# A graph network kernel: one of the dense half-chunks is done in another place of the first layers

## The chip, the cores and the metric

The kernel runs on one core of a Trainium2 chip. It is one program with five instruction streams: VectorE (DVE), ScalarE (ACT), TensorE (PE), GpSimd (POOL) and SyncE (SP). The metric is device time in microseconds, the median over runs; less is better.

## The reference

`x` has 100000 rows of 32 numbers; 25000 edges (`src`, sorted `dst`, a type each) touch some of them. Four layers follow, each `x = x + layer(relu(layernorm(x)))`.

```python
h = relu(layernorm(x)); x = x + norm * (segment_sum((norm * h)[dst], src) + norm * h)      # norm = rsqrt(1 + out degree)
h = relu(layernorm(x)); x = x + sum_k theta[k] * L^k h                                     # L h = h - D^-1/2 A D^-1/2 h, k = 0..4
h = relu(layernorm(x)); x = x + relu(sum over edges of gate * message + self term)         # typed messages, at dst
h = relu(layernorm(x)); x = x + ten steps of 0.9 * norm * segment_sum((h * norm)[src], dst) + 0.1 * h
```

A node that no edge touches has no neighbours, so all four layers act on its row alone: three layer norms (the third with its factor for the last layer) and three additions. This is the *dense* part. The kernel computes it for all 100000 rows, and afterwards overwrites the rows that have edges.

## The kernel before

**Dense part.** The rows are cut into a small tail and 20 chunks of 128 partitions by 39 rows (1248 numbers, 0.64 MB). Two chunks make a *half*, and there are ten halves, numbered 0 to 9. `dense_half` on VectorE (with `dense_pair`, lines 1311 to 1357) does three rounds of the same layer norm: sum, centre, [ScalarE squares, L2135], sum of squares, [ScalarE roots, L2138], reciprocal, scale, add. ScalarE also issues a half's two loads and, as its chunks are done, its two stores (`dense_halves` of ScalarE, L2149 to L2166). ScalarE loads one half ahead within a group of halves: it waits for the stores of half n - 1, issues the loads of half n + 1, and only then does the squares and roots of half n. The first load of a group is issued when VectorE raises `dense_go`.

**Where the halves are.** The halves are put by hand into the order of the irregular work:

- *early* (0 to `MIDDLE_HALF` - 1), after the tail: while GpSimd scatters the sums of nodes with many edges (L1902) and then gathers the source rows `xs` (L1896), with at most four source gathers in flight.
- *middle* (up to `ROUNDS_HALF` - 1), after `dense_go` at L1447: while GpSimd gathers own and first rows of the listed edges.
- *rounds* (up to `LATE_HALF` - 1): one after the second `l1_step` (L1504, L1505), one after the last step (L1511).
- *late* (from `LATE_HALF` on), in another tile, after L1514.

**Between early and middle.** `source_norm(part)` and `first_layer` compute the first layer for three parts of the source rows (columns 0 to 104, 104 to 150, 150 to 196), and each waits for its part's gathers. After each part SyncE stores its own rows (L527). Then come two listings, the clear at L1422 and L1423 that lets GpSimd gather own rows, a layer norm, the first rows (stored by SyncE at L530), and `Z`, the rows that SyncE stores as x_rows (L548). VectorE waits for the store of the first rows and for the store of x_rows (`s2_stored`); the latter because it clears the third rows' tile `m3_f`, a part of `z_t`, which that store reads. It computes the coefficients `cf` (L618 and L1443 here) and goes on to the middle halves.

**After the middle.** VectorE takes own and first rows, makes the carried sums (scan L1214), lists again (`compact_listed`) and raises `l1_second_ready` (L1473). SyncE stores the second and the own listed rows, GpSimd gathers 14 columns of each, and VectorE goes on at L1480 and L1482. Three `l1_step`s follow; the first two end in a store of third rows and 14 gathers of them, with half of a scatter of 50 columns of finished rows behind each.

All waits are on semaphores and each engine's order is the order of the code; no planner moves anything.

Of the kernel before, what the change touches and what calls it, by code (L numbers as in the profile page):

```python
# [69 lines left out]

UNROLL = 4
TURNS = DCHUNKS // UNROLL
MIDDLE_HALF, ROUNDS_HALF, LATE_HALF, HALVES = 3, 5, 7, 2 * TURNS


def build(nc, x, src, dst, etype, theta, w_basis, w_comp, w_self, a1t, a1b, a2t, a2b, rel, out):
# [12 lines left out]
    V, S, T, G = nc.vector, nc.scalar, nc.tensor, nc.gpsimd  # L89
# [20 lines left out]
    with ctx:  # L110
        def sb(name, cols, dt=f32, parts=P):
            return ctx.enter_context(nc.sbuf_tensor(name, [parts, cols], dt))

        def sem(name):
            return ctx.enter_context(nc.semaphore(name))
# [89 lines left out]
        small = sb("small", 4)  # L205
# [44 lines left out]
        EARLY_IN, LATE_IN, MIDDLE_IN, ROUNDS_IN = range(4)  # L250
# [39 lines left out]
        m3_f = z_t[:, 5 * CW2:6 * CW2]  # L290
# [141 lines left out]
        s = {n: sem(n) for n in SEMS}  # L432
# [22 lines left out]
        def bc(ap, n=D):  # L455
            return ap.unsqueeze(2).to_broadcast([ap.shape[0], ap.shape[1], n])

        def bf(ap, n=EC):
            return ap.unsqueeze(1).to_broadcast([ap.shape[0], n, ap.shape[1]])
# [150 lines left out]
        def _(dve):  # L610
            link = Chain(dve, s["dve"])
            marks.clear()

            def tt(o, a, b, op):
                return V.tensor_tensor(o, a, b, op)  # L615

            def ts(o, a, s1, s2, op0, op1=None):
                return V.tensor_scalar(o, a, s1, s2, op0, op1) if op1 is not None else V.tensor_scalar(o, a, s1, None, op0)  # L618
# [594 lines left out]
            def sums_of(chain, w, m, z, cont, carry_in, number):  # L1213
                chain.many([V.tensor_tensor_scan(z[:, :, f], cont, m[:, :, f], 0.0, ALU.mult, ALU.add) for f in range(D)])  # L1214
                V.tensor_copy(last_row, z[:, w - 1, :]).then_inc(s[carry_in], 1)
                dve.wait_ge(s[carry_in], number)
# [132 lines left out]
            def turn_half(i, h, chain, place):  # L1349
                dve.wait_ge(s[f"dense_in{h}"], 32 * i + 32)  # L1350
                dense_pair([2 * h, 2 * h + 1], P, DCH, chain, lambda l, b: 12 * i + (3 + 6 * h + 2 * l + b + 1), place)

            def dense_half(n, place):
                turn_half(n // 2, n % 2, Chain(dve, s["dense_chain"], tail_chain.n + n * PER // 2), place)

            def dense_halves(first, last, place):
                for n in range(first, last):
                    dense_half(n, place)
                dve.wait_ge(s["dense_done"], 2 * last + 1)
# [71 lines left out]
            dve.wait_ge(s["s2_ready"], 1)  # L1431
            dve.wait_ge(s["l1_first_ready"], 1)
            dve.wait_ge(s["l1_first_stored"], 16)
            dve.wait_ge(s["s2_stored"], 16)
            link(V.memset(m3_f, 0.0))

            th = [theta_sb[:, k:k + 1] for k in range(L1_STEPS + 1)]
            cf = [coef[:, k:k + 1] for k in range(2 * L1_STEPS)]
# [7 lines left out]
            dve.wait_ge(s["l1_own_stored"], 16 * len(XS_PARTS))  # L1446
            V.memset(small[:, 2:3], 0.0).then_inc(s["dense_go"], 1)  # L1447
            dense_halves(MIDDLE_HALF, ROUNDS_HALF, MIDDLE_IN)
            dve.wait_ge(s["l1_own_in"], 16 * W1)
            x1c = OWN1[:, :, 0:D]  # L1450
            link(V.tensor_copy(disc, OWN1[:, :, D]))
# [15 lines left out]
            with dve.If(longest <= XW):  # L1467
                ch = Chain(dve, s["l1c_chain"])
                w2 = W2S["l1"]
                m2, own2, m3, z2, t2, u2 = (a[:, 0:w2, :] for a in (M2, OWN2, M3, Z2, T2, U2))  # L1470
                cn2, hd2, ds2 = (a[:, 0:w2] for a in (cont2, head2, dis2))

                V.tensor_copy(small[:, 2:3], small[:, 1:2]).then_inc(s["l1_second_ready"], 1)  # L1473
                V.scalar_tensor_tensor(out=x1c, in0=Zc, scalar=cf[0], in1=x1c, op0=ALU.mult, op1=ALU.add).then_inc(s["l1_listed_ready"], 1)
                dve.wait_ge(s["l1_listed_ready"], 1)
                ch(ts(valid1, SECOND[:, :, D], FAR / 2, FAR, ALU.is_lt, ALU.mult))
                ch(tt(nohome, nohome, valid1, ALU.add))
                ch(tt(homei, OWN1[:, :, D + 2], nohome, ALU.add))
                dve.wait_ge(s["l1_second_in"], 16 * w2)
                ch(V.tensor_copy(pf3[:, 0:w2], m2[:, :, D]))  # L1480
                dve.wait_ge(s["l1_listed_in"], 16 * w2)
                ch(V.tensor_copy(ds2, own2[:, :, D]))  # L1482
                O2 = own2[:, :, 0:D]
                base_n = ch.n
                PER2 = 1 + 4

                def l1_step(i, m):
                    ch = Chain(dve, s["l1c_chain"], base_n + i * PER2)
                    sums_of(ch, w2, m, z2, cn2, "l1c_carry_in", i + 1)
                    dve.wait_ge(s["l1c_carry_out"], i + 1)  # L1490
                    ch(tt(t2, bf(CAR, w2), bc(hd2), ALU.mult))
                    ch(tt(z2, z2, t2, ALU.add))
                    ch(tt(z2, z2, bc(ds2), ALU.mult))
                    if i < L1_STEPS - 2:
                        tt(u2, z2, bc(ds2), ALU.mult).then_inc(s["l1_third_ready"], 1)
                    ch(V.scalar_tensor_tensor(out=O2, in0=z2, scalar=cf[i + 1], in1=O2, op0=ALU.mult, op1=ALU.add))
                    assert ch.n == PER2

                l1_step(0, m2)
                for i in range(1, L1_STEPS - 1):  # L1500
                    dve.wait_ge(s["l1_third_in"], 16 * w2 * i)
                    l1_step(i, m3)
                    if i == 1:
                        V.memset(small[:, 2:3], 0.0).then_inc(s["dense_go"], 1)  # L1504
                        dense_half(ROUNDS_HALF, ROUNDS_IN)  # L1505
                ch = Chain(dve, s["l1c_chain"], base_n + (L1_STEPS - 1) * PER2)
                ch(tt(home2i[:, 0:w2], own2[:, :, D + 2], away2[:, 0:w2], ALU.add))
                V.tensor_copy(small[:, 2:3], small[:, 3:4]).then_inc(s["x2c2_ready"], 1)

                V.memset(small[:, 1:2], 0.0).then_inc(s["s_final"], 1)  # L1510
                dense_half(ROUNDS_HALF + 1, ROUNDS_IN)  # L1511
                dve.wait_ge(s["dense_done"], 2 * LATE_HALF + 1)
                dve.wait_ge(s["s_final"], 1)
                V.memset(small[:, 2:3], 0.0).then_inc(s["dense_go"], 1)  # L1514
                dense_halves(LATE_HALF, HALVES, LATE_IN)
# [741 lines left out]
        def _(pe):  # L2257
# [37 lines left out]
            def place(layout, wo, nv):  # L2295
                for g, (cut, hot, _, given) in enumerate(layout):
                    n = cut.stop - cut.start
                    placed[0] += 1
                    pe.wait_ge(s["place_in"], placed[0])
                    for q in range(n):  # L2300
                        ins = T.matmul(PLACED[:, 0:2 * nv * wo], hot[:, q, :], given[:, q, :, :].rearrange("p d c -> p (d c)"),
                                       start=g == 0 and q == 0, stop=g == len(layout) - 1 and q == n - 1)
                    ins.then_inc(s["place_out"], 1)
# [133 lines left out]
```

## Time and profile before

| | |
|---|---|
| median of 3 runs | 2403.41 us (2403.01 to 2404.06) |
| the profiled execution's own time | 2400.89 us |
| its span, first to last instruction | 2399.1 us |
| VectorE busy | 1839.2 us, 77% of the span |
| GpSimd busy | 1445.9 us, 60% |
| ScalarE, TensorE busy | 386.9 us, 336.3 us |

The page also has the chain of work that ended last. Here it covers the end of the program, from 1967 us on, mostly GpSimd's gathers and scatters. The stages that the diff touches lie between 600 and 1560 us; they are read in the timelines, where each row has a start (us from the span's start), a duration, the engine, the line of the code, the operation with its tiles, and in brackets how long the engine had been idle before it and what released it. A line such as L615 or L1896 is a helper's, so the tile tells which work it is.

### The profile page before, as it was taken

Reading aid. Unit: us, or ns where it says so; the run is one execution under the profiler, and the core shown is the slowest. Engines: PE = TensorE matmul, PEld = TensorE weight load, DVE = VectorE, ACT = ScalarE, POOL = GpSimd, SP = SyncE. Lnnn points to the kernel's source line nnn. Section 1 sums busy time; section 2 is a strip of 40 time slices with the busy share of each in tenths; the row PEclk is TensorE's granted clock in tenths of the full one; section 3 lists DMA queues with packets and bytes.
Section 4 is the critical chain, followed back from the end, with each engine's and each line's share of the span. In section 5 each row is a group of like instructions: output and inputs, shape, how many; then the busy total and the mean of one; then the engine's idle time right before and its main releaser. Section 6 shows DMA issues by size and latency. Waiting matters only on the chain. (4 is left out here: it accounts for less than half of the span.)

```text
span 2399.1 us, 13018 instructions
## 1 busy us (share of the span) xinstructions
PE 336.3 (14%) x2316; PEld 248.2 (10%) x2316; DVE 1839.2 (77%) x3276; ACT 386.9 (16%) x1277; POOL 1445.9 (60%) x1429
## 2 busy tenths in 40 slices
PE   0000000202000010000000001117615750001430
PEld 0000000201000010000000001004413430001430
DVE  8998989899789985993398998999999997133110
ACT  0000002020111101210011120127716751000000
POOL 6666776372667117703677770087677665777775
PEclk9999999999999999999999999996655665555555
DMA  1001003010131105201102121000001002101000
GB/s 21 16 9 30 12 16 122 6 12 4 53 109 55 48 16 201 48 21 33 56 28 73 53 97 66 0 7 9 8 31 40 7 7 69 12 9 36 11 12 7
DMA packets 58030, 88.43 MB, mean 37 GB/s; under 512 B 26485, under 2 KB 49992, under 8 KB 56312
## 3 DMA queue, kind: packets, MB, share of 16 engines
q0 software_dynamic: 44960, 19.03, 5.3%
q1 hardware_dynamic: 7160, 43.31, 4.6%
q10 hardware_dynamic: 5856, 25.60, 2.8%
q14 instruction: 49, 0.40, 0.1%
q8 instruction: 5, 0.08, 0.0%
HBM read 37.41 MB, written 54.81 MB: 38 GB/s over the span
## 5 line engine op out<-in xcount | busy, mean ns | idle before, releaser
L1902 POOL DMA_INDIRECT out<-outs,i_src x196 | 223.3, 1139 | 188.7 <-DVE outs L1623 114.8
L1896 POOL DMA_INDIRECT xd<-in_x,i_dst x196 | 205.7, 1050 | 108.7 <-DVE mf L615 55.1
L1896 POOL DMA_INDIRECT xs<-in_x,i_outS x196 | 196.0, 1000 | 71.5 <-issue 57.0
L615 DVE TENSOR_TENSOR mf<-mf 128x128 f32<-128x128 f32 (+6 forms) x582 | 180.9, 348 | 10.5
L2135 ACT ACTIVATE pay<-pay 128x1248 f32<-128x1248 f32 (+1 forms) x63 | 75.5, 1199 | 612.4 <-DVE pay L1321 583.7
L615 DVE TENSOR_TENSOR pay<-psum,pay 128x512 f32<-128x512 f32 x196 | 130.5, 684 | 17.7 <-ACT pay L2225 15.8
L1647 DVE TENSOR_REDUCE z<-pay 128x512 f32 (+1 forms) x196 | 132.3, 675 | 0.0
L2368 PE MATMUL psum<-pay 128*128 128x512 f16 x196 | 106.3, 543 | 143.3 <-ACT pay L2210 101.3
L1902 POOL DMA_INDIRECT out<-outs,i_srcX x100 | 104.3, 1043 | 32.9 <-issue 28.3
L1902 POOL DMA_INDIRECT out<-z,i_srcX x96 | 94.6, 986 | 40.8 <-DVE z L1647 24.3
L1896 POOL DMA_INDIRECT mf<-l_own_rows,lists x50 | 49.9, 997 | 111.1 <-DVE mf L1423 96.2
L1335 DVE SCALAR_TENSOR_TENSOR psum<-pay,psum 128x1248 f32<-128x1248 f32 (+1 forms) x63 | 88.7, 1407 | 2.2
L1896 POOL DMA_INDIRECT mf<-l_second_rows,nsrc x26 | 25.9, 998 | 101.2 <-DMA l_second_rows<-mf 93.5
L1902 POOL DMA_INDIRECT sums_by_edge<-mf,edge x46 | 45.2, 983 | 66.0 <-DVE mf L615 52.3
L1320 DVE TENSOR_REDUCE psum<-outs 128x39 f32<-128x1248 f32 (+1 forms) x45 | 62.0, 1378 | 20.9 <-DMA outs<-in_x 20.3
L1896 POOL DMA_INDIRECT mf<-payload_by_dst,edge x46 | 45.8, 996 | 48.0 <-DVE mf L1251 34.3
L2358 PE MATMUL psum<-ident,pay 128*128 128x128 f16 x197 | 56.4, 286 | 97.3 <-ACT pay L2202 97.3
L615 DVE TENSOR_TENSOR outs<-outs,psum 128x1248 f32<-128x1248 f32 (+2 forms) x55 | 68.5, 1258 | 1.6
L1321 DVE SCALAR_TENSOR_TENSOR pay<-psum,outs 128x1248 f32<-128x1248 f32 (+1 forms) x45 | 62.1, 1380 | 1.6
L2282 PE MATMUL psum<-small,upper 128*128 128x1 f32 x18 | 5.3, 362 | 406.3 <-DVE small L1028 406.3
L2102 ACT ACTIVATE outs<-pay 128x3136 f32<-128x3136 f32 x6 | 16.9, 2817 | 274.6 <-DVE pay L646 274.6
L1896 POOL DMA_INDIRECT mf<-l_first_rows,lists x50 | 49.8, 996 | 15.2 <-issue 15.2
(565 smaller groups left out, 2743.1 us busy)
## 6 DMA issues: line engine op xcount, KB each, us to landing
outs<-in_x ACTq DMA_DIRECT2D x14, 624.0 KB, 5.3
out<-outs ACTq DMA_DIRECT2D x14, 624.0 KB, 3.0
z<-in_x ACTq DMA_DIRECT2D x6, 624.0 KB, 6.0
out<-z ACTq DMA_DIRECT2D x6, 624.0 KB, 2.9
payload_by_dst<-z SPq DMA_DIRECT2D x1, 3234.0 KB, 9.6
sums_by_edge<-z SPq DMA_DIRECT2D x1, 3234.0 KB, 17.3
z<-sums_by_edge SPq DMA_DIRECT2D x1, 3234.0 KB, 13.7
l_first_rows<-mf SPq DMA_DIRECT2D x1, 3234.0 KB, 9.6
```

The source lines that it names most:

```text
L615: return V.tensor_tensor(o, a, b, op)
L1320: chain(V.tensor_reduce(dense_m[b][0:pn, 0:cn], X3, AX.X, ALU.add))
L1321: V.scalar_tensor_tensor(out=rows(dxc[b][0:pn, 0:w]), in0=bc(dense_m[b][0:pn, 0:cn]), scalar=-1.0 / D, in1=X3, op0=ALU.mult, op1=ALU.add). ...
L1335: chain(V.scalar_tensor_tensor(out=rows(h), in0=rows(dxc[b][0:pn, 0:w]), scalar=0.0, in1=bc(scale), op0=ALU.max, op1=ALU.mult))
L1647: V.tensor_reduce(Z[:, bass.ds(t, 1), :], prod[slot].rearrange("p (o b) -> p o b", b=NBAS).unsqueeze(1), AX.X, ALU.add).then_inc(s["l2_don ...
L1896: G.indirect_dma_start(out=dest(k), out_offset=None, in_=table, in_offset=bass.IndirectOffsetOnAxis(ap=idx[:, k:k + 1], axis=0), bounds_ch ...
L1902: G.indirect_dma_start(out=table, out_offset=bass.IndirectOffsetOnAxis(ap=idx[:, k:k + 1], axis=0), in_=source(k), in_offset=None, bounds_ ...
L2102: S.activation(hout[:, side, :], tmp[:, side, :], ACT.Square).then_inc(s["norm_squared"], 1)
L2135: S.activation(dsq[b][0:pn, 0:w], dxc[b][0:pn, 0:w], ACT.Square).then_inc(s["dense_sq"], 1)
L2282: T.matmul(CAR[:, 0:1], upper[:], small[:, 3:4], start=True, stop=True)
L2358: T.transpose(XXTp[b % 2], xxc[b], ident16[:])
L2368: T.matmul(PWm[b % 2], xxt[b], w_both, start=True, stop=True)
```

## The change

`MIDDLE_HALF` and `ROUNDS_HALF` go down by one: early has halves 0 and 1, middle 2 and 3. `dense_go` for the rounds is raised, and one half (4) done, between `l1_listed_ready` and the wait for the second rows. The other two places of the rounds stay, with halves 5 and 6, and the `dense_go` of the first of them is gone. The wait for `s2_stored` and the clear of `m3_f` move from ahead of the coefficients to behind the middle halves.

```diff
-MIDDLE_HALF, ROUNDS_HALF, LATE_HALF, HALVES = 3, 5, 7, 2 * TURNS
+MIDDLE_HALF, ROUNDS_HALF, LATE_HALF, HALVES = 2, 4, 7, 2 * TURNS
...
             dve.wait_ge(s["l1_first_stored"], 16)
-            dve.wait_ge(s["s2_stored"], 16)
-            link(V.memset(m3_f, 0.0))
...
             dense_halves(MIDDLE_HALF, ROUNDS_HALF, MIDDLE_IN)
+            dve.wait_ge(s["s2_stored"], 16)
+            link(V.memset(m3_f, 0.0))
             dve.wait_ge(s["l1_own_in"], 16 * W1)
...
                 dve.wait_ge(s["l1_listed_ready"], 1)
+                V.memset(small[:, 2:3], 0.0).then_inc(s["dense_go"], 1)
                 ch(ts(valid1, SECOND[:, :, D], FAR / 2, FAR, ALU.is_lt, ALU.mult))
                 ch(tt(nohome, nohome, valid1, ALU.add))
                 ch(tt(homei, OWN1[:, :, D + 2], nohome, ALU.add))
+                dense_half(ROUNDS_HALF, ROUNDS_IN)
                 dve.wait_ge(s["l1_second_in"], 16 * w2)
...
                     if i == 1:
-                        V.memset(small[:, 2:3], 0.0).then_inc(s["dense_go"], 1)
-                        dense_half(ROUNDS_HALF, ROUNDS_IN)
+                        dense_half(ROUNDS_HALF + 1, ROUNDS_IN)
...
-                dense_half(ROUNDS_HALF + 1, ROUNDS_IN)
+                dense_half(ROUNDS_HALF + 2, ROUNDS_IN)
```

## Rows read from the trace of the kernel before

**Rows 1.** The page, busy time: us, share of the span, instructions.

```profile
PE 336.3 (14%) x2316; PEld 248.2 (10%) x2316; DVE 1839.2 (77%) x3276; ACT 386.9 (16%) x1277; POOL 1445.9 (60%) x1429
```

**Rows 2.** Waits of VectorE: us in total, times, longest.

```profile
DVE nsrc L1480 <- DMA mf<-l_second_rows,nsrc: 20.7, 1, 20.7
```

**Rows 3.** Timeline of VectorE, early halves to the last source norm.

```profile
684.96 2.81 DVE L1325 TENSOR_REDUCE mf<-pay 128x39 f32<-128x1248 f32 x2 [7.93 <-ACT pay L2135]
...
725.57 1.45 DVE L1320 TENSOR_REDUCE psum<-outs 128x39 f32<-128x1248 f32 x1
...
772.05 3.63 DVE L644 TENSOR_REDUCE psum<-xs 128x104 f32<-128x3328 f32 x1
...
828.70 1.70 DVE L644 TENSOR_REDUCE psum<-xs 128x46 f32<-128x1472 f32 x1
```

**Rows 4.** Timeline of GpSimd: the last source gather and the next instruction.

```profile
791.73 1.08 POOL L1896 DMA_INDIRECT xs<-in_x,i_outS  x1 [0.30 <-issue]
888.98 0.99 POOL L1896 DMA_INDIRECT mf<-l_own_rows,lists  x1 [96.17 <-DVE mf L1423]
```

**Rows 5.** Tile xs on GpSimd, 667 to 795: idle time before, and landing.

```profile
  DMA xs<-in_x,i_outS: 6.5, 3
...
DMA to landing us min/median/max: 2.3/2.4/10.5
```

**Rows 6.** Timeline of VectorE around the middle halves.

```profile
951.48 0.43 DVE L1435 MEMSET z<- 128x448 f32 x1 [19.20 <-DMA x_rows<-z]
...
953.88 0.06 DVE L1447 MEMSET small<- 128x1 f32 x1
959.76 1.46 DVE L1320 TENSOR_REDUCE psum<-outs 128x39 f32<-128x1248 f32 x1 [5.82 <-DMA outs<-in_x]
...
1063.33 5.16 DVE L1214 TENSOR_TENSOR_SCAN pay<-lists,mf 128x50 f32<-128x50 f32 x32
```

**Rows 7.** Timeline of GpSimd: last first rows, last third rows, first send.

```profile
1017.81 1.00 POOL L1896 DMA_INDIRECT mf<-l_first_rows,lists  x1 [0.30 <-issue]
...
1227.28 0.99 POOL L1896 DMA_INDIRECT z<-l_third_rows,nsrc  x1 [0.30 <-issue]
...
1558.40 3.51 POOL L1902 DMA_INDIRECT out<-outs,i_src  x1 [114.84 <-DVE outs L1623]
```

**Rows 8.** Timeline of VectorE in the rounds.

```profile
1108.42 1.88 DVE L1474 SCALAR_TENSOR_TENSOR mf<-pay,lists,mf 128x1600 f32<-128x1600 f32 x1
...
1149.91 0.17 DVE L1482 COPY nsrc<-mf 128x14 f32<-128x14 f32 x1 [17.99 <-DMA mf<-l_own_listed_rows,nsrc]
...
1186.03 0.06 DVE L1504 MEMSET small<- 128x1 f32 x1
1191.69 1.46 DVE L1320 TENSOR_REDUCE psum<-outs 128x39 f32<-128x1248 f32 x1 [5.60 <-DMA outs<-in_x]
...
1238.07 3.22 DVE L1214 TENSOR_TENSOR_SCAN z<-nsrc,z 128x14 f32<-128x14 f32 x32
```

**Rows 9.** Tile z, 668 to 670: SyncE's load of the sums.

```profile
L543 SPq DMA_DIRECT2D z<-sums_by_edge x1: 320/320/320, 668.6 to 668.6; - x1
...
DMA to landing us min/median/max: 13.7/13.7/13.7
```

**Rows 10.** Tile l_first_rows, 920 to 926: SyncE's store of the first rows.

```profile
L530 SPq DMA_DIRECT2D l_first_rows<-mf x1: 319/319/319, 925.0 to 925.0; - x1
...
DMA to landing us min/median/max: 9.6/9.6/9.6
```

**Rows 11.** Tile out, 667 to 674: ScalarE's two dense stores of half 0.

```profile
L2166 ACTq DMA_DIRECT2D out<-outs x2: 350/350/351, 668.0 to 671.3; - x2
...
DMA to landing us min/median/max: 3.3/7.4/11.4
```

**Rows 12.** DMA queues, 920 to 965: packets, MB, share of the engines.

```profile
q1 hardware_dynamic: 432, 9.73, 52.6%
q10 hardware_dynamic: 576, 2.56, 15.4%
```

## The prediction

> **What bounds the kernel now.** I read the page first: VectorE is busy for 77% of the span, and no other engine for more than 60% [rows 1]. The stage the diff touches (600 to 1560 us) lies ahead of the part that the page's chain follows, so I went on to the waits of VectorE. In this stretch its long waits are the one for the second rows [rows 2] and those in the timelines below. Then I read the timeline of VectorE, with that of GpSimd beside it, from the end of one wait to the next. The reader should see three places.
>
> Early. Three halves run back to back. The second stalls 7.93 us and gives way to the third at 725.57; that one lasts until 772.05, 46.48 us without a wait. The layer that follows never waits for source rows: its last part starts at 828.70, at once [rows 3]. GpSimd issues the last source gather at 791.73 [rows 4], and such a gather lands 2.4 us after issue (median) [rows 5]. So VectorE is 34.6 us later than its data, and GpSimd then idles 96.17 us until VectorE's clear at L1423 [rows 4]. VectorE sets the time here.
>
> Middle. VectorE sits 19.20 us until the store of x_rows has landed, only to clear the tile of the third rows; then it asks for dense input at 953.88 and gets it at 959.76. After the halves, the scan at 1063.33 needs first rows of which the last were asked for at 1017.81 [rows 6, 7]. VectorE sets the time here too, with some 43 us of slack on the other side.
>
> Rounds. VectorE waits 20.7 and 17.99 us [rows 2, 8] for the second and the own listed rows, idle. After the second step it asks for dense input at 1186.03, has it at 1191.69, and one half fills the wait for the third rows until 1238.07 [rows 8]. Later GpSimd idles 114.84 us before its first send at 1558.40, released by VectorE [rows 7]. What VectorE gains up to there reaches the end, if nothing after it is bound to a clock of its own.
>
> **The change, part by part.** There are still ten halves. (The branch for long lists is not taken here.)
>
> 1. One early half leaves: 46.48 us of VectorE. The stall of 7.93 us goes as well: ScalarE sat behind the wait for half 0's stores so that it could load half 2 before squaring half 1, and with MIDDLE_HALF = 2 there is no half 2 to load. VectorE reaches the source norms at 772.05 - 46.48 - 7.93 = 717.6. The part from 772.05 to 828.70 takes 56.7 us, so it would reach the last part at 774.3 [rows 3]. The sums (issued at 668.6, 13.7 us to land [rows 9]) and half 1's stores are there long before. But the last source row lands at 791.73 + 2.4 = 794.1, so VectorE now waits some 20 us: this is what is late next. One thing is new: the stores of the own rows, which before were issued when all gathers were done, now run beside the last thirty or so. Beside a bulk load and a dense store the gathers took up to 10.5 us to land and cost GpSimd 6.5 us in three stalls [rows 5]. The own rows are smaller (104 of 196 columns first, the rest in two short stores), and four gathers may be in flight, so I take 2 us. Gain: 828.70 - 796.1 = 32.6, between 28.1 (the whole 6.5) and 34.6 (nothing). GpSimd's gathers of own rows move with VectorE.
>
> 2. The clear of the third rows' tile moves behind the middle halves. The clear itself (0.43 us) is paid in either place. The wait is what counts. VectorE still waits for the store of the first rows, which lands 9.6 us after issue at 925.0, so at 934.6 [rows 10]; the coefficients take 2.0 us (951.91 to 953.88), and the request goes out at 936.6 instead of 953.88 [rows 6]. At that time the two other stores of SyncE have until 951.4 to run. SyncE's queue moves 9.73 MB between 925.0 and then [rows 12], 370 GB/s; at that rate the two loads of the first half (1.28 MB) need 3.4 us. Alone, request to first use is 5.9 us [rows 6]. How does a dense transfer fare beside a bulk one? The second dense store of half 0, issued at 671.3, landed after 11.4 us, its twin ahead of it after 3.3 [rows 11], while the 3.2 MB load of the sums was in flight until 682.3 [rows 9]: it came through only as the bulk ended. The packets show why that can be: 9.73 MB in 432 packets on SyncE's queue, 2.56 MB in 576 on ScalarE's [rows 12], 22.5 against 4.4 KB; turn by turn the small ones get a sixth. So I take "when the bulk is through": 951.4 + 3.4 and some 0.8 for landing = 955.6, a gain of 959.76 - 955.6 = 4.2 us. Bounds: 2.5, if the load starts only when the store has landed (951.4 + 5.9); 13.9, if both share evenly (5.9 + 3.4 after 936.6 = 945.9). The store of x_rows lands some 3 us later at most, and its first reader is now 90 us away.
>
> On this the Trainium skill (DMA: Bandwidth & Descriptors, Queues, rings and completion order) says that each DMA engine goes round the queues that have work and drains a packet of some 9 to 17 descriptors from one before it turns to the next. With nothing said of bytes it leaves open whether the turns are even in time; even turns would make the middle term 13.9 instead of 4.2. The trace, with 11.4 us for the second store, speaks for uneven ones.
>
> 3. A half moves into the wait for the second rows. The request goes out after L1474, at 1108.42 + 1.88 = 1110.3 [rows 8]. With 5.66 us for the load, as at 1186.03, it starts at 1116.0 and ends 46.4 later at 1162.4; two copies later the first step starts at 1162.8, where it started at 1150.1: 12.7 late. The wait of 38.7 us is too short for load and half. Its load also runs beside SyncE's stores of second and own listed rows (50 slots of 33 and of 35 floats on 128 partitions, 1.7 MB, issued just before), for which I add 1.5: 14.2 late. Bounds: 12.7 and 18 (a load that takes twice as long). ScalarE loads four chunks here, the pair for the next half too, and the pair after that once this half's stores have landed; all that is far from its use. Nothing waits behind this half on VectorE but the step. GpSimd gathers second and own listed rows under it, then waits for the step's third rows, 14.2 later than now.
>
> 4. The next half follows the second step without a request: its input has been there for 35 us. That gives 5.66 back. It ends 46.4 after the step: 1186.0 + 46.4 = 1232.4 on the old scale; the last gather of the second third rows is issued at 1227.28 [rows 7] and lands by 1229.8, so it is still covered, by 2.6 us, as both move by 14.2. VectorE's lateness from here is 14.2 - 5.7 = 8.5. GpSimd's scatters stay 14.2 late, but it waits for VectorE next at 1558.40 with 114.84 us in hand.
>
> Sum: -32.6 - 4.2 + 14.2 - 5.7 = **-28.3 us**. The profiled execution took 2400.9 (its span 2399.1, and 1.8 around it), which gives 2372.6. The median of the timed runs, 2403.4, lies 2.5 above it; against that, **2375.1**.
>
> **Rivals.**
> - *Even sharing in the middle.* The loads come at 945.9. For it: I have only one like case, a store beside a load and not a load beside stores; against it is that case. Sum -38.0: 2365.
> - *Gathers beside a half run slower.* Now 28 gathers run with VectorE idle; then with VectorE at work. The last one lands at 1149.9 [rows 8] and the half ends at 1162.4, so each may slip by 0.45 us for nothing. If each took twice its 1.00 us, the last would land at 1177.9 and the step start 15.5 us after the forecast. Against: the first rows were gathered under the middle halves, at 1.00 us and 0.30 between two [rows 7]. Sum -12.8: 2390.6. The Trainium skill (SBUF — State Buffer, SBUF: two separate sides) has a rule to this effect: a VectorE operation in a two-port mode shuts GpSimd out, and descriptors stall. The trace shows no sign of it under the dense operations.
> - *GpSimd's side becomes the bound later.* It is only 32.6 + 4.2 - 14.2 = 22.6 us earlier, VectorE 28.3. Against: the 114.84 us of slack. Sum -22.6: 2380.8.
> - *The source rows, not VectorE, set the first layer.* This is the one that ends slower. If the last row landed at 828.7 or later, term 1 would be nothing, and what remains is -4.2 + 14.2 - 5.7 = +4.3: 2407.7, and up to +9.8 with the bounds of terms 2 and 3. The sign turns where it lands after 824.4. That takes 30 us of new stalls in the gathers beside the own rows' stores, where a larger transfer cost 6.5.
> - *No change*: only if two of these meet.
>
> **How the numbers follow.** Forecast 0.74, even sharing 0.12, slower gathers 0.05, GpSimd 0.04, rows 0.04 (over 0.2% in part of its span), no change 0.01. The low end is the even sharing, with a little: 2364. The high end takes the bad bound of each term (-28.1 - 2.5 + 18 - 5.7 = -18.3, and 2.6 more should the cover of the third rows in term 4 be gone): 2387.7, which holds GpSimd's case too. 0.2% (4.8 us) is about what can be told from no change. Faster 0.94, same 0.03, slower 0.03.
>
> **What would show it.** Term 1: two early halves, no stall of 8 us in the second, a wait of some 20 us for xs rows before the last source norm, that norm at 796. Term 2: the request 2 us after the first rows' store, a wait for outs of some 19 us in place of 5.8, no wait for x_rows; the halves starting 37 us earlier than now. Term 3: a load wait near 7 us, a half, the step some 14 us further from L1474 than now, no wait for second rows. Term 4: no load wait after the second step. A wait for xs rows far over 20 us would break term 1, a load of 9 us in the middle term 2, a half of over 60 us from request to end term 3.

## The result, and the profile after

The changed kernel takes **2374.3 us** (median of 4 runs, 2372.29 to 2375.66) against 2403.2 for the kernel before: ratio 0.9882, 95% interval [0.9868, 0.9896], 28.9 us less. Its profiled execution took 2372.29 us with a span of 2370.5, which is 28.6 under the span of before. The forecast was 2375.1, in a range of 2364 to 2387.7.

The page, busy time of the engines in the changed kernel (us, share, instructions): the same work as in [rows 1], in a shorter span.

```profile
PE 327.4 (14%) x2316; PEld 243.1 (10%) x2316; DVE 1841.0 (78%) x3276; ACT 386.6 (16%) x1277; POOL 1445.6 (61%) x1429
```

Five of the longer waits of VectorE in the changed kernel (us in total, times, longest). The wait for the second rows [rows 2] and those for x_rows [rows 6] and the own listed rows [rows 8] are no longer there. The new ones are the wait for xs rows, the 19.4 us among those for the dense input, and one of 2.5 us for the store of the first rows.

```profile
DVE psum L1320 <- DMA outs<-in_x: 36.3, 4, 19.4
DVE tmp L618 <- DMA mf<-l_second_rows,nsrc: 30.8, 1, 30.8
DVE z L1214 <- DMA z<-l_third_rows,nsrc: 21.7, 1, 21.7
DVE z L618 <- DMA z<-l_link_rows,linksi: 20.5, 1, 20.5
DVE psum L644 <- DMA xs<-in_x,i_outS: 19.8, 1, 19.8
```

(The second and fourth of these belong to the last layer; both kernels have them.) The timeline of VectorE in the changed kernel, with the instructions that answer to [rows 3], [rows 6] and [rows 8]: the first and the last source norm, the dense request and its first use, the clear in its new place and the scan, L1474 with the new request, the first step, the second, and the third.

```profile
717.75 3.63 DVE L644 TENSOR_REDUCE psum<-xs 128x104 f32<-128x3328 f32 x1
...
794.66 1.69 DVE L644 TENSOR_REDUCE psum<-xs 128x46 f32<-128x1472 f32 x1 [19.82 <-DMA xs<-in_x,i_outS]
...
902.40 0.06 DVE L1445 MEMSET small<- 128x1 f32 x1
921.84 1.46 DVE L1320 TENSOR_REDUCE psum<-outs 128x39 f32<-128x1248 f32 x1 [19.38 <-DMA outs<-in_x]
...
1014.81 0.43 DVE L1448 MEMSET z<- 128x448 f32 x1 [0.16 <-DVE outs L615]
...
1026.01 5.15 DVE L1214 TENSOR_TENSOR_SCAN pay<-lists,mf 128x50 f32<-128x50 f32 x32
...
1071.12 1.88 DVE L1474 SCALAR_TENSOR_TENSOR mf<-pay,lists,mf 128x1600 f32<-128x1600 f32 x1
1073.06 0.06 DVE L1476 MEMSET small<- 128x1 f32 x1
1081.88 1.46 DVE L1320 TENSOR_REDUCE psum<-outs 128x39 f32<-128x1248 f32 x1 [8.12 <-DMA outs<-in_x]
...
1128.67 3.06 DVE L1214 TENSOR_TENSOR_SCAN z<-nsrc,mf 128x14 f32<-128x14 f32 x32
...
1157.67 3.14 DVE L1214 TENSOR_TENSOR_SCAN z<-nsrc,z 128x14 f32<-128x14 f32 x32 [21.73 <-DMA z<-l_third_rows,nsrc]
...
1211.44 3.23 DVE L1214 TENSOR_TENSOR_SCAN z<-nsrc,z 128x14 f32<-128x14 f32 x32
```

Set against the kernel before, this gives a ledger. Each line is how far the point has moved; the difference between two lines is one term.

| point | before | after | moved | term, measured | forecast |
|---|---|---|---|---|---|
| last source norm | 828.70 | 794.66 | -34.0 | 1: -34.0 | -32.6 |
| L1474 | 1108.42 | 1071.12 | -37.3 | 2: -3.3 | -4.2 |
| first step | 1150.12 | 1128.67 | -21.4 | 3: +15.9 | +14.2 |
| third step | 1238.07 | 1211.44 | -26.6 | 4: -5.2 | -5.7 |
| first send, next group | 1558.40 | 1530.93 | -27.5 | -0.9 | 0 |
| span | 2399.1 | 2370.5 | -28.6 | -1.1 | 0 |

GpSimd in the changed kernel: the own rows' gathers follow VectorE's clear as in [rows 4], and before the first send it still has 108 us in hand, as in [rows 7].

```profile
854.65 1.00 POOL L1897 DMA_INDIRECT mf<-l_own_rows,lists  x1 [61.48 <-DVE mf L1423]
...
1530.93 3.51 POOL L1903 DMA_INDIRECT out<-outs,i_src  x1 [108.08 <-DVE outs L1624]
```

### The profile page after: what moved, and what is told of

The parts are those of the page before. It is cut to its first block and busy times, and to the rows that moved or that the text cites. A ratio compares the mean times of both kernels' runs of the same rounds, so it can differ in the third digit from the quotient of the medians.

```text
span 2370.5 us, 13019 instructions
## 1 busy us (share of the span) xinstructions
PE 327.4 (14%) x2316; PEld 243.1 (10%) x2316; DVE 1841.0 (78%) x3276; ACT 386.6 (16%) x1277; POOL 1445.6 (61%) x1429
## 5 line engine op out<-in xcount | busy, mean ns | idle before, releaser
L1903 POOL DMA_INDIRECT out<-outs,i_srcX x100 | 104.0, 1040 | 33.1 <-issue 28.3
L1903 POOL DMA_INDIRECT x_rows<-mf,lists x50 | 50.2, 1003 | 15.2 <-issue 15.2
```

Source lines behind the costliest of these rows:

```text
L1903: G.indirect_dma_start(out=table, out_offset=bass.IndirectOffsetOnAxis(ap=idx[:, k:k + 1], axis=0), in_=source(k), in_offset=None, bounds_ ...
```

## The experiments

The changed kernel and its variants are compared with the kernel before through runs of both on one chip; the ratios are compared across the sets of runs, since the kernel before itself had medians of 2400.2 to 2403.2.

**Ten runs, in one view.**

| run | median us | before, same chip | ratio [95%] |
|---|---|---|---|
| the changed kernel again | 2375.2 | 2401.9 | 0.9889 [0.9873, 0.9906] |
| clear put back | 2374.9 | 2400.2 | 0.9899 [0.9884, 0.9914] |
| clear moved alone | 2397.5 | 2400.2 | 0.9988 [0.9979, 0.9997] |
| wait for second rows left empty | 2411.0 | 2400.2 | 1.0044 [1.0029, 1.0060] |
| half to the middle | 2415.0 | 2401.9 | 1.0054 [1.0037, 1.0071] |
| both stores behind the load | 2360.1 | 2400.2 | 0.9837 [0.9822, 0.9852] |
| x_rows alone behind | 2366.8 | 2401.5 | 0.9851 [0.9834, 0.9867] |
| listings in the wait | 2355.4 | 2401.5 | 0.9807 [0.9790, 0.9823] |
| both of these ideas | 2341.6 | 2401.5 | 0.9750 [0.9734, 0.9767] |
| and the request first | 2339.5 | 2401.5 | 0.9742 [0.9725, 0.9758] |

**The changed kernel again**, no edit.

> The changed kernel once more, beside the kernel before on the same chip: ratio 0.988, and the waits for xs rows, for the middle load and for the load in the rounds at 19.8, 19.4 and 8.1 us again.

The ratio came again. The wait for the middle load was 19.1 us; that for xs rows was 21.1 and that in the rounds 8.8 us, 1.3 and 0.7 over what was expected. The ledger of this run against the kernel before reads -31.9, -3.3, +16.5, -5.3, -1.0 and -1.1, together -26.1 by the spans. Between these two executions of the same kernel term 1 (the last source rows) differs by 2.1 us, the others by 0.7 or less.

**Clear put back, clear moved alone.** Two runs for term 2, from both ends.

```diff
             dve.wait_ge(s["l1_first_stored"], 16)
+            dve.wait_ge(s["s2_stored"], 16)
+            link(V.memset(m3_f, 0.0))
...
             dense_halves(MIDDLE_HALF, ROUNDS_HALF, MIDDLE_IN)
-            dve.wait_ge(s["s2_stored"], 16)
-            link(V.memset(m3_f, 0.0))
```

> The changed kernel with the wait for the store of x_rows and the clear put back ahead of the coefficients. Theory (the dense load comes through only as the bulk stores end): the request goes out 17 us later but is served in 5.9 instead of 19.4 us, so the middle halves start 3.3 us later (the 37.9 us between 959.76 and 921.84, less the 34.0 of the last source norm and the 0.5 us of the clear that is now paid later), time 3.3 over the changed kernel, about 2377.6. Rival (the removed wait was worth most of its 19.2 us): 14 to 17 over it, 2388 to 2391.

The second run is the reverse edit, made on the kernel before:

> The kernel before, with only the wait and the clear moved behind the middle halves. Theory: 3.3 us faster than before, about 2399.9, with a load wait of 19 us in place of 19.2 + 5.8. Rival: 14 us faster, 2389.

The run with the clear put back has ratio 0.9899, and its interval overlaps that of the changed kernel, so its time alone tells only that 14 us are ruled out. Its trace gives the size. From the last source norm (793.16) to the first use of the middle's input (924.04) it takes 130.9 us; in the changed kernel (794.66, 921.84) 127.2. Of the 3.7, 0.5 is the clear's own place, so 3.2 us are the term. The clear moved alone makes the kernel before faster by 0.0012 [0.0003, 0.0021], 2.9 us. Here are VectorE's rows of these two, the one with the clear put back first: 19.24 and 5.60 us of waiting turn into 2.46 and 19.52.

```profile
915.97 0.43 DVE L1435 MEMSET z<- 128x448 f32 x1 [19.24 <-DMA x_rows<-z]
...
924.04 1.46 DVE L1320 TENSOR_REDUCE psum<-outs 128x39 f32<-128x1248 f32 x1 [5.60 <-DMA outs<-in_x]
```

```profile
935.02 0.15 DVE L618 TENSOR_SCALAR lists<-theta_sb 128x1 f32<-128x1 f32 x1 [2.46 <-DMA l_first_rows<-mf]
...
956.54 1.46 DVE L1320 TENSOR_REDUCE psum<-outs 128x39 f32<-128x1248 f32 x1 [19.52 <-DMA outs<-in_x]
```

**Both stores behind the load.** This one takes the bulk away from beside the load and leaves everything else.

```diff
-            sp.dma_start(by_dst, xd_t[:]).then_inc(s["y_table"], 16)
             sp.wait_ge(s["s2_ready"], 1)
+            sp.wait_ge(s["dense_in0"], 64)
+            sp.dma_start(by_dst, xd_t[:]).then_inc(s["y_table"], 16)
             sp.dma_start(x2_dram...).then_inc(s["s2_stored"], 16)
```

> The changed kernel; SyncE issues its stores of the destination rows and of x_rows only when the first middle half's load has landed. Theory (bulk transfers beside the load make it slow): the load wait falls from 19.4 to 6 to 8 us and the time by 11 to 13, to about 2362; the stores are needed only 90 us later. Rival (it is the own rows' gathers or the place in the program that make it slow): wait stays near 19 and the time at 2374.

The load wait fell from 19.4 to 5.4 us, and the ratio from 0.9882 to 0.9837, 11 us (13.7 by the spans of the two profiled executions). GpSimd's gathers of own rows ran beside the load as before (50 of them, from 855 to 919 us), so they are not what slowed it. VectorE's rows:

```profile
902.97 0.06 DVE L1446 MEMSET small<- 128x1 f32 x1
908.41 1.46 DVE L1321 TENSOR_REDUCE psum<-outs 128x39 f32<-128x1248 f32 x1 [5.38 <-DMA outs<-in_x]
```

**x_rows alone behind.** As above, but the store of the destination rows stays where it was.

> The changed kernel; only the store of x_rows waits for the first middle half's load, that of the destination rows stays ahead of it. Theory (the load comes through when the bulk ahead of it is through, here some 8 us after the request): load wait 10 to 13 us, 7 to 9 us faster than the changed kernel, between it and the run in which both stores waited. Rival (x_rows alone, reading the tile and bank beside, is what slows the load): wait near 6, 13 us faster, like the run with both behind.

The load wait was 11.2 us, the ratio 0.9851, 7 us under the changed kernel: between the two, as the theory has it. In this run the store of the destination rows took 18.7 us to land, the loads 10.9 (median); the load came through some 4 us after that one store had ended.

```profile
904.49 0.06 DVE L1446 MEMSET small<- 128x1 f32 x1
915.77 1.46 DVE L1321 TENSOR_REDUCE psum<-outs 128x39 f32<-128x1248 f32 x1 [11.22 <-DMA outs<-in_x]
```

**Wait for second rows left empty.** Half 4 leaves its new place and stands ahead of half 5, behind the second step.

```diff
-                V.memset(small[:, 2:3], 0.0).then_inc(s["dense_go"], 1)
...
-                dense_half(ROUNDS_HALF, ROUNDS_IN)
                 dve.wait_ge(s["l1_second_in"], 16 * w2)
...
                     if i == 1:
+                        V.memset(small[:, 2:3], 0.0).then_inc(s["dense_go"], 1)
+                        dense_half(ROUNDS_HALF, ROUNDS_IN)
                         dense_half(ROUNDS_HALF + 1, ROUNDS_IN)
```

> The changed kernel with half 4 taken out of the wait for the second rows and put ahead of half 5 behind the second step. Theory (VectorE's order is the bound, the wait for the second rows is worth 38.7 us of cover, and the wait for the third rows already has a half over it): first step 37.3 us earlier than before, then two halves in a row, third step 9 us later than before; time 35 to 36 over the changed kernel, about 2410. Rival (gathers run slower beside a half, so that the cover was worth less): clearly under 30 over it.

The first step started at 1112.57 and the third at 1247.37, 9.3 us later than before, where 9 were forecast. The ratio is 1.0044, 39 us above the changed kernel by ratio (1.0044 - 0.9882; 37 by its second set of runs, 0.9889), where 35 to 36 were expected. The third step is 35.9 us behind that of the changed kernel; the rest has no named cause. VectorE's rows show the two waits of the kernel before, back at their old lengths.

```profile
1094.16 0.17 DVE L1480 CAST nsrc<-mf 128x14 int32<-128x14 f32 x1 [20.88 <-DMA mf<-l_second_rows,nsrc]
1112.36 0.17 DVE L1482 COPY nsrc<-mf 128x14 f32<-128x14 f32 x1 [18.02 <-DMA mf<-l_own_listed_rows,nsrc]
```

**Half to the middle.** The kernel before with `MIDDLE_HALF = 2` and `ROUNDS_HALF = 5`.

> The kernel before with MIDDLE_HALF = 2 alone: one half goes from the early place to the middle, where no wait is to be filled; clear and rounds as before. Theory (an early half is worth 34.0 us there, a stall of 7.9 us included, and a half on VectorE's path costs its 46.5 us): 12.5 us slower than before, about 2413 to 2414, with no stall of 8 us in the middle, since no bulk load runs beside its stores. Rival (the middle has room, as GpSimd is 43 us ahead there but its gathers once waited for VectorE): no slower than before.

It is 13.1 us slower than before (ratio 1.0054). The last source norm is at 795.36 and the first step at 1163.76, 13.6 us later than before. VectorE has no wait of 8 us for ScalarE there.

**Listings in the wait.** The block from `lead0, given0` to the pointers `leadF`, `edgeF` is moved between the second part and the third.

```diff
-            for part in range(1, len(XS_PARTS)):
+            for part in (1,):
                 source_norm(part)
                 first_layer(*XS_PARTS[part])
             lead0, given0 = ...
...
             pointers(ids, ..., ((0, leadF), (1, edgeF)))
+            for part in (2,):
+                source_norm(part)
+                first_layer(*XS_PARTS[part])
```

> The changed kernel; the two listings that stand behind the last source norm (some 40 us of VectorE and TensorE that need none of the source rows) come ahead of it, so they fill the wait of 19.8 us for the last rows. Theory (that wait is real time on VectorE's path, and it is what the early half's removal could not turn into gain): 19 to 20 us faster than the changed kernel, about 2354, no wait for xs rows. Rival (what follows is bound by GpSimd or by the stores of own rows, so the wait is free): within 3 us of the changed kernel.

The ratio went from 0.9882 to 0.9807, 18 us (0.9889 for the changed kernel's second set: 20). The last source norm now stands behind the listings, at 814.84, with no wait ahead of it, and the clear of `kept` follows at 830.71, where it was at 850.54.

```profile
774.64 0.06 DVE L1400 MEMSET small<- 128x1 f32 x1
...
814.84 1.70 DVE L644 TENSOR_REDUCE psum<-xs 128x46 f32<-128x1472 f32 x1
...
830.71 3.69 DVE L1425 MEMSET mf<- 128x4352 f32 x1 [0.86 <-issue]
```

**Both, and the request first.** The edits of "both stores behind" and "listings in the wait" together; then, on top, the request for the rounds' first load one instruction earlier.

> The changed kernel with both: the listings ahead of the last source norm, and both of SyncE's stores behind the first middle half's load. Theory (two separate places of one chain): the gains add, 19.5 + 12, about 2342. Rival (with VectorE 31 us earlier the gathers of first rows become the bound, which had some 40 us in hand): the second gain is cut, over 2348.

> As the run with both, and the dense request of the half in the wait for second rows is raised ahead of the addition at L1474, 1.9 us earlier. Theory (that load shares the engines with SyncE's stores of second and own listed rows by need of both): the half starts 1 to 2 us earlier and the time is 1 to 2 us less than with both. Rival (it delays the store of second rows and so the gathers, or is served as late as before): no change against the run with both.

Both together give 2341.6, ratio 0.9750: 31.7 us under the changed kernel by ratio, the sum of the two parts' (18 and 11) and a little more. The load wait is 5.9 us. The gathers of first rows have not become the bound: the last is issued at 964.25, and VectorE does not wait for it. The request first gives 2339.5; its interval overlaps that of "both", so the time leaves it open. In its trace the way from L1474 to the first use is 8.2 us (1039.17 to 1047.41) instead of 10.8 (1038.54 to 1049.36), 2.6 us shorter.

## Why the prediction was right

The sum was -28.3 us and the measured one is -28.6 by the spans, -28.9 by the medians. The four terms, too, were right in place, sign and size, none off by more than 1.7 us. That the sums agree to 0.3 us is in part luck: the four terms together were 1.7 us too good, 2.0 us that were not forecast at all made up for it, and the second profiled execution of the changed kernel gives -26.1.

- **Term 1** (early half out, -34.0 for -32.6). VectorE came to the source norms at 717.75 (717.6 forecast) and waited 19.8 us for the last rows. I had taken 2 us of stalls for the own rows' store beside the gathers; the trace shows one stall of 1.1 us at 766. The 54.4 us that left this place brought 34.0. The run with the listings in the wait shows that the rest was real time on VectorE's path: fill it with work that was due anyway, and it comes back.
- **The stall of 7.93 us** was put down to ScalarE's order of loads and squares. It is gone as forecast. The traces show that it took two things. In the changed kernel half 0's second store is as slow as before, 11.1 us to land beside the load of the sums, but no load of half 2 waits for it, and there is no stall. The middle of the run with three halves there has the same order of loads and squares, its first stores land after 3.0 us, and there is no stall either. The prediction named the order; the store's 11.4 us [rows 11] is the other half of the cause.
- **Term 2** (clear and its wait, -3.3 for -4.2). The wait of 19.2 us and the load wait of 5.8 turned into waits of 2.5 and 19.4. The clear itself I had called neutral and yet had counted the request without it: those 0.5 us are over half of the error. The cause stands: with both stores away the load takes 5.4 us, with one beside it 11.2, with two 19.4. The rival of even sharing is out, for it had 9.3 us for the changed kernel. "When the bulk is through" was too plain a rule, though. The first chunk, asked for at 902.5, landed after 14.9 us, while x_rows' store was still under way until 920.2; that store took 22.2 us to land, where it took 18.9 before, and the half was in use 1.6 us behind it, not 4.2. So the load does move beside the bulk, slowly, and holds it up by 3 us: a small share. That the unequal packets of [rows 12] are the reason for it is argued, and no run changed a packet's size. The Trainium skill (DMA: Bandwidth & Descriptors, Queues, rings and completion order) has each DMA engine switch queues packet by packet. By these waits the turns are not alike in time: alike, they would give some 9.3 us (the prediction's estimate) beside one store or two, and 11.2 and 19.4 were measured.
- **Term 3** (a half into the wait for second rows, +15.9 for +14.2). The load beside SyncE's stores took 8.8 us from request to first use, not 7.2, and that is the whole difference. The half itself took 46.4.
- **Term 4** (no second request, -5.2 for -5.7). The 5.7 came back; the wait for the first third rows was 0.5 longer (21.7). The second third rows were covered.
- **After the rounds** another 2.0 us were gained that the prediction did not have: 1.3 in the load wait of the late halves (7.35 for 8.62), 0.7 of no named cause. The repeat has 2.2, with a wait of 7.32. Whether they belong to the change is open: other runs with the half in the new place had late waits of 7.9 to 8.5 us.
- **The other rivals.** Slower gathers are out: the 28 gathers under the half have the same median as with VectorE idle, 997 ns. This is the view by tile of GpSimd's gathers under the half, with the durations in ns (least, median, most):

```profile
L1897 POOL DMA_INDIRECT mf<-l_second_rows,nsrc x14: 992/997/1000, 1075.4 to 1092.3; - x14
L1897 POOL DMA_INDIRECT mf<-l_own_listed_rows,nsrc x14: 992/997/999, 1093.6 to 1110.5; - x14
```

GpSimd as the later bound is out with 108 us in hand. The source rows as the bound of the first layer, the slower case, did come in, but as forecast only for the last 20 us of the gain.

What carried the gain is the pair of places: "half to the middle" has the same early gain and no empty wait to put the half into, and is 13 us slower than before; "wait for second rows left empty" is 11 us slower. Of the places tried, the half pays only in the 38.7 us wait.

## What to carry to other kernels

Work moved out of one place gains only down to the next arrival, here the last source row, so look at once for other work that can take what is left of that wait: it was worth two thirds as much as the change. A wait for a store that is taken away may come back as the wait for whatever is loaded next, since the store is still in flight: order the transfers by who needs them first, and let a store that nobody reads for long go last. Filling a wait of 38.7 us with 46.4 us of work and its load is still worth it if the same work costs all of its length elsewhere.

## What the runs showed of the hardware that was not expected

The mean granted clock of TensorE differed between executions that took the same time. In the profiled executions of the kernel before and of most others it was 0.85; in that of the changed kernel it was 0.70, and the run with the listings in the wait and the one with both had 0.69. The windows show where. In the changed kernel the granted clock fell from 1.00 (2.4 GHz) to 0.50 (1.2 GHz) between 830 and 835 us, at the end of TensorE's work of 824 to 833 us, before which it had been idle for 219 us. It came back near 1590. In the repeat, the same kernel, it stayed at 1.00 through the same work. The columns are the stretch, its length in us, TensorE's busy time and matmuls, clock, DMA share and GB/s; the changed kernel first, then the repeat.

```profile
825.00:830.00 5.00, 2.61 (x38) 1.00 0.02 3
830.00:835.00 5.00, 1.22 (x4) 0.59 0.00 0
835.00:840.00 5.00, 0.00 (x0) 0.50 0.00 0
960.00:1580.00 620.00, 23.98 (x146) 0.50 0.15 49
```

```profile
830.00:835.00 5.00, 1.71 (x6) 1.00 0.00 0
835.00:840.00 5.00, 0.31 (x2) 1.00 0.00 0
960.00:1580.00 620.00, 23.99 (x146) 1.00 0.15 49
```

So the same 146 matmuls have the same busy time at either level. Timed executions of the changed kernel at 0.85 took 2374.0 to 2375.7 us, the one at 0.70 took 2372.3: the lower clock cost nothing that can be seen here. Why it fell in some executions and not in others stays open, and so does why the busy time did not change with it.
